# Attention stage: row scores by single heads in two banks, transposed scores in a ring of four, and another order of the query tiles

## The reference, cut to what matters

```
q = (h @ Wq.T).reshape(bsz, q_len, 32, 16)     # 32 query heads of 16
k, v: the same with 8 heads                     # each shared by 4 query heads
q, k = rope(q), rope(k)
logits = einsum('bhqd,bhkd->bhqk', q, k) / 4
logits = where(causal, logits, finfo.min)
attn = softmax(logits, axis=-1)
x = x + (einsum('bhqk,bhkd->bhqd', attn, v)) @ Wo.T
```

## Time and profile before

| | us |
|---|---|
| median of three runs | 2697.47 |
| the profiled execution's own time | 2699.94 |
| its span, first to last instruction | 2698.1 |
| attention, first row score to the last addition to x | 2342.41 to 2593.10 |

### The profile page before, as it was taken

How to read it: one execution, slowest core, us unless ns; L and a number is a source line. 1 busy time by engine, 2 the same in 40 slices (tenths; PEclk the granted TensorE clock), 3 DMA queues, 4 the chain that set the end, 5 groups by cost and what they waited for, 6 DMA issues and landing times. The chain is left out here.

```text
span 2698.1 us, 32843 instructions
## 1 busy us (share of the span) xinstructions
PE 2403.2 (89%) x12160; PEld 1851.6 (69%) x12160; DVE 1718.1 (64%) x2342; ACT 1302.0 (48%) x1884; POOL 1332.2 (49%) x877
## 2 busy tenths in 40 slices
PE   4995699999999999999999999998699857889955
PEld 3873578778778778788788788786477633566623
DVE  4554578578588588588588588585456345664325
ACT  2311467467467467477477477475232022235521
POOL 1222189579589489489499499497222100000000
PEclk9997799999999999999999999998799967999986
DMA  3420333233223233233233233231153002000000
GB/s 98 102 84 5 99 98 110 86 98 110 86 94 110 90 95 118 82 104 115 75 106 110 78 106 110 75 106 60 36 116 97 27 14 73 1 2 2 2 14 31
DMA packets 163542, 204.12 MB, mean 76 GB/s; under 512 B 24408, under 2 KB 86360, under 8 KB 163256
## 3 DMA queue, kind: packets, MB, share of 16 engines
q1 hardware_dynamic: 163384, 202.02, 24.9%
HBM read 198.49 MB, written 3.15 MB: 75 GB/s over the span
## 5 line engine op out<-in xcount | busy, mean ns | idle before, releaser
L1601 POOL TENSOR_TENSOR mamba_w_lo<-mamba_raw,mamba_w_hi 128x512 fp32r<-128x512 f32 x272 | 435.1, 1608 | 293.5 <-ACT mamba_w_hi L1465 293.5
L76 PE MATMUL psum<-mamba_hT_lo,mamba_w_hi 128*128 128x512 f32 x1152 | 461.9, 401 | 6.3 <-POOL mamba_w_lo L1601 6.3
L77 PE MATMUL psum<-mamba_hT_hi,mamba_w_hi 128*128 128x512 f32 x1152 | 456.3, 396 | 0.0
L78 PE MATMUL psum<-mamba_hT_hi,mamba_w_lo 128*128 128x512 f32 x1152 | 456.3, 396 | 0.0
L1620 POOL TENSOR_SCALAR mamba_L<-mamba_A,mamba_ts 128x256 f32<-128x256 f32 (+1 forms) x256 | 333.0, 1315 | 0.1
L1718 DVE TENSOR_TENSOR mamba_L<-mamba_L,mamba_cb 128x1536 f32<-128x1536 f32 x128 | 309.0, 2414 | 21.8 <-ACT mamba_L L1514 13.9
L1686 DVE SCALAR_TENSOR_TENSOR mamba_hid<-psum,mamba_cw,mamba_hid 128x1022 f32<-128x1022 f32 (+2 forms) x192 | 245.1, 1277 | 21.4 <-ACT mamba_hid L1472 16.8
L76 PEld LDWEIGHTS psum<-mamba_hT_lo,mamba_w_hi 128*128 128x128 f32 x1152 | 217.0, 188 | 56.6 <-POOL mamba_w_lo L1601 6.7
L78 PEld LDWEIGHTS psum<-mamba_hT_hi,mamba_w_lo 128*128 128x128 f32 x1152 | 217.0, 188 | 52.5
L77 PEld LDWEIGHTS psum<-mamba_hT_hi,mamba_w_hi 128*128 128x128 f32 x1152 | 217.2, 189 | 49.2
L350 POOL TENSOR_TENSOR ffn_w_lo<-ffn_deq,ffn_w_hi 128x512 fp32r<-128x512 f32 (+2 forms) x66 | 84.3, 1277 | 298.0 <-ACT ffn_w_hi L360 298.0
(11 more groups left out here) (286 smaller groups left out, 5040.8 us busy)
## 6 DMA issues: line engine op xcount, KB each, us to landing
mamba_A<-mamba_a_dram SPq DMA_DIRECT2D x128, 512.0 KB, 4.6
mamba_raw<-in_win SPq DMA_DIRECT2D x144, 256.0 KB, 2.6
mamba_raw<-in_wout SPq DMA_DIRECT2D x128, 256.0 KB, 2.6
mamba_Eb<-mamba_e_dram SPq DMA_DIRECT2D x128, 128.0 KB, 3.0
ffn_raw<-in_w SPq DMA_DIRECT2D x80, 128.0 KB, 3.5
ffn_scl<-in_s SPq DMA_DIRECT2D x80, 128.0 KB, 3.8
ffn_scl<-in_s SPq DMA_DIRECT2D x86, 64.0 KB, 2.3
ffn_raw<-in_w SPq DMA_DIRECT2D x20, 256.0 KB, 2.6
```

Source lines behind the costliest of these rows:

```text
L76: e.matmul(out, wh, ml, start=start, stop=False)
L77: e.matmul(out, wh, mh, start=False, stop=False)
L78: return e.matmul(out, wl, mh, start=False, stop=stop)
L1601: e.tensor_tensor(w.lo[:, k % NSPLIT, :], raw[:, k % NRAW, :], w.hi_read[:, k % NSPLIT, :], ALU.subtract).then_inc(s["w_lo"], 1)
```

## The change

Row scores are made by single heads: head k uses bank k % 2 and waits until head k - 2 is read. Each head has its own maximum instruction, so a step has 32 of them in place of 16. Transposed scores use banks 2 to 5 in turn and wait for exponential k - 4. The order of the query tiles becomes 0, 0, 2, 2, 3, 3, 1, 1, so steps have 2, 2, 6, 6, 8, 8, 4 and 4 quads. The single heads of step s + 2 are spread over the quads of step s by the same rule.

```diff
-    STEPS = [(b, qt) for qt in reversed(range(QT)) for b in range(SEQS)]
+    STEPS = [(b, qt) for qt in (0, 2, 3, 1) for b in range(SEQS)]
...
-            return [(s + 2, z) for z in range(i * NQ // n, (i + 1) * NQ // n)]
+            return [(s + 2, *divmod(k, 2)) for k in range(i * NH // n, (i + 1) * NH // n)]
...
-                def score(s, z):
+                def score(s, z, h):
                     b, qt = STEPS[s]
-                    k, n = s * NQ + z, P * (qt + 1)
+                    k, n = s * NH + 2 * z + h, P * (qt + 1)
                     if k >= 2:
                         e.wait_ge(peaked, k - 1)
-                    for h in range(2):
-                        e.matmul(psum[:, 2 * (k % 2) + h, 0:n], qs[:, b, z, qt * P:(qt + 1) * P],
-                                 ks[:, b, 2 * (z // QPK) + h, 0:n], start=True, stop=False)
-                    for h in range(2):
-                        last = e.matmul(psum[:, 2 * (k % 2) + h, n - P:n], identr[:], maskr[:], start=False, stop=True)
-                    last.then_inc(scored, 1)
+                    e.matmul(psum[:, k % 2, 0:n], qs[:, b, z, qt * P:(qt + 1) * P],
+                             ks[:, b, 2 * (z // QPK) + h, 0:n], start=True, stop=False)
+                    e.matmul(psum[:, k % 2, n - P:n], identr[:], maskr[:], start=False, stop=True).then_inc(scored, 1)
...
-                    if k >= 2:
-                        e.wait_ge(exped, k - 1)
+                    if k >= 4:
+                        e.wait_ge(exped, k - 3)
...
-                    out = ps[4 + k % 2].rearrange("p (h q) -> p h q", h=QPK)
+                    out = ps[2 + k % 4].rearrange("p (h q) -> p h q", h=QPK)
...
-                    e.activation(pt[:, k % NPT, :], ps[4 + k % 2], ACT.Exp, scale=SCALE).then_inc(exped, 1)
+                    e.activation(pt[:, k % NPT, :], ps[2 + k % 4], ACT.Exp, scale=SCALE).then_inc(exped, 1)
...
-                    e.tensor_reduce(mx[:, s % 2, :].rearrange("p (h z) -> p h z", h=2)[:, :, z],
-                                    psum[:, 2 * (k % 2):2 * (k % 2) + 2, 0:n], AX.X, ALU.max).then_inc(peaked, 1)
+                    e.tensor_reduce(mx[:, s % 2, h * NQ + z:h * NQ + z + 1], psum[:, k % 2, 0:n], AX.X, ALU.max
+                                    ).then_inc(peaked, 1)
```

More of the change, by code:

```diff
@@ L826, in place @@
                                  stop=True).then_inc(placed, 1)
-                def score(s, z):
+                def score(s, z, h):
                     b, qt = STEPS[s]
-                    k, n = s * NQ + z, P * (qt + 1)
+                    k, n = s * NH + 2 * z + h, P * (qt + 1)
                     if k >= 2:
                         e.wait_ge(peaked, k - 1)
-                    for h in range(2):
-                        e.matmul(psum[:, 2 * (k % 2) + h, 0:n], qs[:, b, z, qt * P:(qt + 1) * P],
-                                 ks[:, b, 2 * (z // QPK) + h, 0:n], start=True, stop=False)
-                    for h in range(2):
-                        last = e.matmul(psum[:, 2 * (k % 2) + h, n - P:n], identr[:], maskr[:], start=False, stop=True)
-                    last.then_inc(scored, 1)
+                    e.matmul(psum[:, k % 2, 0:n], qs[:, b, z, qt * P:(qt + 1) * P],
+                             ks[:, b, 2 * (z // QPK) + h, 0:n], start=True, stop=False)
+                    e.matmul(psum[:, k % 2, n - P:n], identr[:], maskr[:], start=False, stop=True).then_inc(scored, 1)
                 def turn_maxima(s):
-                    e.wait_ge(peaked, (s + 1) * NQ)
+                    e.wait_ge(peaked, (s + 1) * NH)
                     wait_spare()
@@ L916, in _ @@
                 for s in range(2):
-                    for z in range(NQ):
-                        score(s, z)
+                    for k in range(NH):
+                        score(s, *divmod(k, 2))
                     turn_maxima(s)
@@ L1032, in keep, with peak @@
                         e.tensor_copy(stack(b, z), ps[z % 4]).then_inc(st_dve, 1)
-                def peak(s, z):
-                    k, n = s * NQ + z, P * (STEPS[s][1] + 1)
+                def peak(s, z, h):
+                    k, n = s * NH + 2 * z + h, P * (STEPS[s][1] + 1)
                     e.wait_ge(scored, k + 1)
@@ L1072, in _ @@
                 for s in range(2):
-                    for z in range(NQ):
-                        peak(s, z)
+                    for k in range(NH):
+                        peak(s, *divmod(k, 2))
                     low_maximum(s)
```

## The result

| | before | changed |
|---|---|---|
| median of five runs, us | 2699.07 (2696.51 to 2701.67) | 2715.93 (2713.05 to 2719.55) |
| span of the profiled execution | 2698.1 | 2714.1 |
| attention stage | 250.7 | 265.6 |

The changed kernel is slower: its runs against those of before give a ratio of 1.006, 95% interval 1.0048 to 1.0072, which is 13 to 19 us. Of the 16.0 us between the two spans, 14.9 lie between the first row score (2343.26) and the last addition to x (2608.87). The rest, about 1 us, lies almost wholly ahead of the stage, whose start differs by up to 6 us from kernel to kernel in the profiles of this study.

What follows compares the result with a forecast made beforehand. DVE was taken to bound the stretch ahead of the loop, PE the loop, with turns through bank 7 stopping PE. Terms 32 + 177.2 + 50.7 + 9.1 = 269.0 against 250.7 gave 2715.5 us, range 2694 to 2732.

Steps and rivals of the forecast that it cites:

- the round trip: Row scores: product, maximum and hand-overs, shared by two heads in two banks; 0.42, 0.50, 0.59, 0.69 us per head by width.
- masked transposed scores: Steps 0 and 1: each takes 0.53 us on PE against 0.22 of slack, adding 0.7 us per quad.
- ahead of the loop: Before the loop over quads: 64 heads of 128 columns take 32 us, between 29.1 and 35.5 at the lower clock.
- quads of steps 0 and 1: Four quads with 64 heads of 384 columns: 11.4 us each, 47 us with 2 us for a low clock.
- quads of steps 2 and 3: Twelve quads with 64 heads of 512 columns: eight at 4.4 us, four at 5.3, 56.4 us in all.
- quads of steps 4 and 5: Sixteen quads with 64 heads of 256 columns: 3.1 us unmasked, 4.0 masked, 53.2 in all; ring gives 7.
- quads of steps 6 and 7: Eight quads without row scores: 5.1 us per pair of quads, 20.6 us in all.
- turns and output products: Turns through bank 7 and output products in the loop, with new collisions in the short first steps: 50.7 us.
- Two banks are enough: Rival, faster: little of a head's wait shows behind PE's other work; -2 us, down to -7 (2690.5); chance 0.12.
- About the same: Rival: maxima overlap by 0.09 us, products hide the remaining wait, clock holds; +3 us, 2700.5; chance 0.15.
- The lower clock persists: Rival: PE stays at the lower clock through steps 0 and 1; +35 us, 2732; chance 0.10.
- the ring brings nothing: Rival: ACT or `weigh` hold PE anyway, so steps 4 and 5 stay at 60 us; +25, 2722.5; chance 0.08.

Runs made afterwards that it cites:

- four_banks: Changed kernel with single-head row scores in four banks and transposed scores in two, new tile order; ratio to before 0.9950, stage 238.7 us.
- ahead_four: Changed kernel with single heads in four banks only ahead of the loop over quads, two inside it; ratio to before 0.9971, stage 245.8 us.
- order_only: Kernel before with only the new order of query tiles, pairs of heads in four banks kept; ratio to before 1.0023, stage 260.3 us.
- ring_two: Changed kernel with transposed scores in two banks instead of four, the rest as changed; ratio to before 1.0086, stage 274.2 us.
- four_old: Kernel before with pairs split into single heads in four banks, transposed scores in two, old tile order; ratio to before 0.9980, stage 251.8 us.
- clock_fill: Changed kernel with each 128-column row-score product ahead of the loop run twice; ratio to before 1.0079, stage 272.5 us.

## Why the prediction was right

It gave 2715.5 us and +18; the median was 2715.93 and the difference 16.9. That the median was met to 0.4 us is luck: the stage grew by 14.9 and not by 18.3 (its own sign was 15 to 20), about 1 us came from outside the stage, and the median of before moved from 2697.47 to 2699.07 with two more runs. The mechanism was right in the main: the round trip through two banks costs more than the ring of four gives. Two of its parts were wrong, the price of the masked transposed scores and the share of the ring, and the runs allow the terms to be checked singly.

| term | predicted | measured |
|---|---|---|
| ahead of the loop | 32 | 33.9 |
| quads of steps 0 and 1 | 47 | 41.9 |
| quads of steps 2 and 3 | 56.4 | 57.2 |
| quads of steps 4 and 5 | 53.2 | 52.2 |
| quads of steps 6 and 7 | 20.6 | 21.0 |
| turns and output products | 50.7 | 50.3 |
| tail | 9.1 | 9.1 |
| stage | 269.0 | 265.6 |

The quads are the plain ones from `weigh` to `weigh`: for steps 2 and 3 8 x 4.42 + 4 x 5.46, for steps 4 and 5 12 x 3.03 + 4 x 3.96; for steps 0 and 1 the 45.4 less the turns at quads 2 and 3 as predicted (2.3 and 1.15); for steps 6 and 7 the 34.2 less their six turns at the predicted prices (13.2). These two rows of the table are thus measured only as far as those prices hold. The turns are what is left between 2377.14 and the last `weigh`. The 50.3 holds 16.7 of predicted prices and 0.9 of one `weigh`; where plain quads stand beside the turns, in steps 2 to 5, they took 32.8 against 32.4 predicted. The end of the stage:

```profile
2598.90 1.92 PE L866 MATMUL psum<-attn_hT,attn_v 128*32 128x512 f32 x16
2599.73 0.18 PEld L866 LDWEIGHTS psum<-attn_hT,attn_v 128*32 128x32 f32 x8 [0.68 <-ACT attn_hT L973]
...
2608.18 0.69 DVE L1060 TENSOR_TENSOR s_x<-s_x,psum 128x512 f32<-128x512 f32 x1 [5.25 <-PE psum L896]
```

Maxima of 512 elements in steps 2 and 3, in the changed kernel and in four_banks:

```profile
2466.18 3.38 DVE L1036 TENSOR_REDUCE attn_mx<-psum 128x1 f32<-128x512 f32 x5
...
2433.58 3.07 DVE L1036 TENSOR_REDUCE attn_mx<-psum 128x1 f32<-128x512 f32 x5
```

- **The round trip.** 0.42 per head of 128 columns became 0.41 with the clock up and 0.54 (0.52 predicted) at 1.2 GHz; 0.59 for 384 columns became 0.575 between transposed scores (1.15 for two heads), 0.69 for 512 became 0.67. Groups by shape give 291 ns for 128 elements (293 predicted) and 553 for 384 (560). Four_banks shows that it was this loop, and not DVE's work, that cost the time.
- **The clock ahead of the loop.** The value between the two bounds was taken, and the slow bound came closer: the clock fell within 5 us and stayed down. With the clock up 64 x 0.41 + 2.2 = 28.4, so by this estimate it cost some 5.5 us, and 1.5 more in the first two quads (20.6 instead of the 19.1 of ahead_four). In ahead_four both are gone.
- **Steps 0 and 1, the term that was mis-sized.** It counted 0.7 us per quad for masked transposed scores that the slack could not take. The group of four heads takes 2.36 instead of twice 1.15, so each costs 0.07 and not 0.23. A quad took 10.6, not 11.4; that is 3.2 of the 5.1 us. Another 1.0 is a `weigh` that the prediction counted here and the table counts with the turns. Of the 2 us for a low clock 1.5 came, all at the start; after the long turns the clock was 1.00 (from 2385 on).
- **Steps 2 and 3.** 4.4 and 5.3 became 4.42 and 5.46. Five maxima of 512 elements in a row (the two rows above) stand 0.67 apart with two banks and 0.60 with four, which is DVE's own pace. With four banks the quads still took 4.0 and 5.07. So the two banks cost 0.4 of each, and the rest is DVE's pace for the five or six long row scores that this order puts into each of twelve quads.
- **Steps 4 and 5.** 3.1 and 4.0 became 3.03 and 3.96. The prediction gave the whole gain, 60.2 to 53.2, to the ring of four. The same sum of quads is 58.0 in order_only, 55.2 in ring_two and 52.2 in the changed kernel: 2.2 us are the shorter row scores of this order, 2.8 the single heads, mixed more finely, and 3.0 the ring.
- **The rivals.** "Two banks are enough" is ruled out by four_banks. The rule that it leaned on (the Trainium skill, Perfetto Trace Analysis, Optimizing Scalar/DVE Operations: breaking up instructions of an engine that is not saturated may help others) held where the ring kept its four banks: pairs to singles took 21.6 us from the new order, and 1.9 from the old (without the slower tail of four_old's profile). With two banks in the old order it did not: 9.2 us were lost, with the ring of four thrown in. "About the same" had the overlap of the maxima right (0.08 to 0.09), but the products did not hide the rest of the round trip, and the clock did not hold. "The lower clock persists" through steps 0 and 1 did not happen, "the ring brings nothing" is ruled out by ring_two, which is 8.6 us longer without it.

The prediction treated the change as one sum and did not say what the order does by itself. The study shows both parts to be losses on the kernel before: +9.6 us for the order, +9.2 for the banks, +14.9 together, which is less than their sum.

## What to carry to other kernels

Count a ring's banks against the round trip of one item (producer, hand-over, consumer, hand-over), divided by the pace of the slower engine. Here a round trip of 0.82 us at a pace of 0.22 asks for 3.7 banks (128 columns), 1.15 at 0.465 for 2.5 (384) and 1.34 at 0.60 for 2.2 (512). Two banks were short in all three, but not in steps 4 and 5, where PE sets the pace (68.0 us with two, 68.1 with four). Three were short ahead of the loop (0.27 us per head instead of 0.22 while the clock held) and within 1.3 us of four in steps 2 and 3. Where banks are fewer than that, both engines wait for each other in turn although neither is saturated. Splitting an item in two halves the ring's depth in time unless the number of items in flight is doubled. Where the phases of a loop need different rings, share out the banks by phase: the terms of single phases added up to 0.1 us here.

A merged row of a profile can hide gaps. Whether an engine sets the pace is seen where nothing holds it up: 0.545 us per maximum of 384 elements looked like DVE's own work until four banks brought 0.465.

## What the runs showed of the hardware

- Maxima out of PSUM overlap. In four_banks they start 0.20 us apart for 128 elements and last 0.27 to 0.29, 0.465 for 384 that last 0.55, and 0.60 for 512 that last 0.68. I had taken the duration for the pace.
- TensorE's clock fell from 2.4 to 1.2 GHz within the first 5 us in which 128-column products came in fours every 0.82 us, and stayed there for 34 us although the records show PE busy for 5.00 of 5 us in several of these stretches. It stayed at 2.4 GHz in the same work with four banks, where products started every 0.11 us. With three banks it held for 11 us and then fell, and with pairs it fell as early as in the changed kernel. Each of these kernels was profiled once.
- At the lower clock 128-column products started 0.21 us apart instead of 0.11 where PE set the pace (order_only, clock_fill, four_banks). A single head in two banks cost 0.54 instead of 0.41 us, not twice as much: DVE's maximum lasted 0.29 at either clock.
